# One tile of two transposed whole, two loads held, and the last rows dealt out anew in a kernel for the lower triangles of Gram matrices

## The reference

```python
def reference(r_inputs):                                # (2048, 64, 256) float32
    Z = jnp.einsum('bnd,bmd->bnm', r_inputs, r_inputs)  # 64 x 64 products of rows, for each batch
    li, lj = jnp.tril_indices(64, k=-1)
    return Z[:, li, lj]                                 # (2048, 2016): below the diagonal, row by row
```

## Time and profile before

| | |
|---|---|
| time before, median of 3 runs | 398.48 us (398.1 to 398.72) |
| profiled execution: its own time | 397.29 us |
| profiled execution: span | 395.5 us |
| PE busy | 368.8 us (93%) |
| DVE busy | 370.4 us (94%) |
| ACT, POOL busy | 188.3, 200.3 us (48%, 51%) |
| HBM read and written | 134.22 MB, 16.52 MB: 381 GB/s over the span |

### The profile page before, as it was taken

The page is one execution under the profiler, slowest core; times in us unless marked ns, Lnnn a source line. Parts: engine busy times, 40 slices in busy tenths (PEclk is TensorE's granted clock), DMA queues, the critical chain, the costliest instruction groups (busy, mean ns, idle before and its releaser), DMA issues.

```text
span 395.5 us, 69567 instructions
## 1 busy us (share of the span) xinstructions
PE 368.8 (93%) x33280; PEld 363.7 (92%) x33280; DVE 370.4 (94%) x369; ACT 188.3 (48%) x858; POOL 200.3 (51%) x975
## 2 busy tenths in 40 slices
PE   4389999999999999999999999999999999999960
PEld 4389999999999999999999999999999999999960
DVE  3258899999999999999999999999999999999995
ACT  0021245454545555555555455545554555545572
POOL 2000075482828456382837557282846648282765
PEclk9569999999999999999999999999999999999995
DMA  8999999999999999999999999999999999994307
GB/s 321 423 421 419 423 422 418 380 424 423 416 405 389 427 420 423 398 422 418 411 422 362 426 423 422 416 419 421 413 420 377 427 414 417 385 416 162 114 16 193
DMA packets 21274, 150.99 MB, mean 382 GB/s; under 512 B 2688, under 2 KB 2816, under 8 KB 4864
## 3 DMA queue, kind: packets, MB, share of 16 engines
q1 hardware_dynamic: 18912, 136.81, 85.5%
q10 hardware_dynamic: 2336, 13.94, 8.7%
HBM read 134.22 MB, written 16.52 MB: 381 GB/s over the span
## 4 chain that ended last, share of the span: by engine, by line
DVE 44%; issue 29%; PE 24%; ACT 0%; DVEq 0%; ACTq 0%
DVE x_turned L232 31%; PE bank_set L309 24%; DVE row_halves L249 11%; DVE x_in L256 1%; DVE packed_rows L154 1%; DVE packed_rows L143 0%; ACT packed_rows L143 0%; DVE x_turned L261 0%; DVEq L248 0%; ACT products L336 0%; DVEq L75 0%; DVEq L279 0%; ACTq L332 0%
## 5 line engine op out<-in xcount | busy, mean ns | idle before, releaser
L309 PE MATMUL bank_set<-x_turned 32*64 32x64 f32 x33280 | 368.8, 237 | 13.1 <-issue 11.1
L309 PEld LDWEIGHTS bank_set<-x_turned 32*64 32x64 f32 x33280 | 363.7, 131 | 18.0 <-issue 11.7
L232 DVE STREAM_TRANSPOSE x_turned<-x_in 128x1024 f32<-128x1024 f32 x256 | 295.7, 1207 | 19.3 <-PE bank_set L309 15.6
L154 POOL COPY packed_rows<-row_halves 32x32 f32<-32x32 f32 (+30 forms) x930 | 191.7, 206 | 187.5 <-DVE row_halves L249 149.9
L336 ACT COPY products<-bank_set 128x512 f32<-128x512 f32 x128 | 75.1, 586 | 146.6 <-PE bank_set L309 130.9
L249 DVE STREAM_TRANSPOSE row_halves<-products 128x1024 f32<-128x1024 f32 x60 | 72.2, 1203 | 0.0
L143 ACT COPY packed_rows<-row_halves 128x32 f32<-128x32 f32 (+30 forms) x465 | 61.2, 218 | 12.5 <-DVE row_halves L249 12.3
L149 ACT COPY packed_rows<-row_halves 128x128 f32<-128x128 f32 x240 | 54.1, 300 | 15.0 <-DVE row_halves L249 13.3
L336 ACT ACT_TABLE_LOAD x1 | 1.3, 1283 | 26.0 <-PE bank_set L309 26.0
L154 POOL COPY packed_rows<-x_in 32x32 f32<-32x32 f32 (+30 forms) x31 | 5.0, 212 | 2.2 <-DVE x_in L256 2.2
L256 DVE STREAM_TRANSPOSE x_in<-products 128x512 f32<-128x512 f32 (+1 forms) x5 | 4.6, 995 | 0.0
## 6 DMA issues: line engine op xcount, KB each, us to landing
x_in<-x_dram SPq DMA_DIRECT2D x128, 1024.0 KB, 15.1
y_dram<-packed_rows ACTq DMA_DIRECT2D x20, 504.0 KB, 8.9
y_dram<-packed_rows SPq DMA_DIRECT2D x4, 504.0 KB, 5.0
y_dram<-packed_rows ACTq DMA_DIRECT2D x6, 252.0 KB
y_dram<-packed_rows ACTq DMA_DIRECT2D x24, 63.0 KB
y_dram<-packed_rows SPq DMA_DIRECT2D x1, 380.0 KB
y_dram<-packed_rows ACTq DMA_DIRECT2D x1, 380.0 KB
y_dram<-packed_rows SPq DMA_DIRECT2D x1, 124.0 KB
```

The source lines that it names most:

```text
L154: return copy(packed_rows[first:first + BLOCK, group % 2, :, at + BLOCK:at + i], halves(group)[first + BLOCK:first + HALF, i, :, 0:i - BLOCK])
L232: nc.vector.transpose(x_turned[:, j, chunks].rearrange("p c b s (h u n v) -> p u v (c b s h) n", h=ROWS // BLOCK, u=PAIRS, v=PAIR), x_in[: ...
L309: done = nc.tensor.matmul(bank_sets[j][side * HALF:(side + 1) * HALF, g, slot, :].rearrange("r (n u v) -> r u n v", u=PAIRS, v=PAIR), rows ...
```

## The change

Five edits stand in one diff.

- `PARTIALS` becomes (1, 2): an even tile is turned by one transpose of 2048 elements a partition, and TensorE reads it behind one wait; odd tiles stay in halves.
- `HELD = (3, 4)`: the fourth load waits until tile 0 is turned whole, the fifth until the first half of tile 1 is. The loads behind them on SyncE's queue wait with them.
- `by_few` holds for 9 groups of the 13 that ScalarE stores (all but 0, 4, 8 and 12) in place of 6.
- Behind the last tile ScalarE packs rows 10 to 31, GpSimd rows 5 to 9, VectorE rows 1 to 4. Both sides of the long rows are stored by SyncE; the short rows still leave from SyncE and ScalarE.
- The last tile's copy out of PSUM is split in two, rows 32 to 63 first; the pieces of long rows wait for the first part alone.

```diff
+    HELD = (3, 4)
     LAP = 2
+    PARTIALS = (1, 2)
-    PARTIALS = 2
-    PARTIAL = CHUNKS // PARTIALS
-    LAST_HOME = (GROUPS * PIECES - 2) * 4 + 2
+    BY_POOL = (5, 10)
...
+        def chunks_of(j, h):
+            some = CHUNKS // PARTIALS[j]
+            return range(h * some, (h + 1) * some)
...
+        def wait_last_kept(engine, piece):
+            lap, s = place(TILES - 1)
+            engine.wait_ge(kept[s], (lap + 2) * LAP - (1 if piece < LONG_PIECES else 0))
...
         def by_few(group):
-            return group % 2 == 1 and group <= FEW_UNTIL
+            return group % 4 != 0 and group <= FEW_UNTIL
...
-        def store_last(engine, side):
-            group, long_rows = GROUPS - 1, first_column(BLOCK)
+        def store_last_long(engine):
+            group = GROUPS - 1
             engine.wait_ge(packed_home, group * PIECES + LONG_PIECES)
             engine.wait_ge(packed_across, (group + 1) * LONG_PIECES)
             engine.wait_ge(last_carried, 1)
-            store(engine, group, slice(long_rows, PACKED), WHOLE_SIDES[side:side + 1])
-            engine.wait_ge(packed_home, GROUPS * PIECES - 1)
-            engine.wait_ge(last_packed, 2)
-            store(engine, group, slice(0, long_rows), WHOLE_SIDES[side:side + 1])
+            store(engine, group, slice(first_column(BLOCK), PACKED), WHOLE_SIDES)
+
+        def store_last_short(engine, side):
+            engine.wait_ge(last_packed, 3)
+            store(engine, GROUPS - 1, slice(0, first_column(BLOCK)), WHOLE_SIDES[side:side + 1])
...
                 if t >= IN_RING:
                     lap, j = place(t - IN_RING)
-                    sync.wait_ge(turned[j][PARTIALS - 1], (lap + 1) * LAP)
+                    sync.wait_ge(turned[j][-1], (lap + 1) * LAP)
+                elif t in HELD:
+                    lap, j = place(t - HELD[0])
+                    sync.wait_ge(turned[j][0], (lap + 1) * LAP)
...
-            store_last(sync, 0)
+            store_last_long(sync)
+            store_last_short(sync, 0)
...
-            pool.wait_ge(rows_turned, GROUPS * PIECES - 1)
-            rows = piece_rows(PIECES - 2)
-            for i in range(rows.start + PIECE // 2, rows.stop):
+            pool.wait_ge(rows_turned, GROUPS * PIECES)
+            for i in range(*BY_POOL):
                 last = pack_short(nc.gpsimd.tensor_copy, GROUPS - 1, i)
...
-                for h in range(PARTIALS):
-                    chunks = slice(h * PARTIAL, (h + 1) * PARTIAL)
+                for h in range(PARTIALS[j]):
+                    chunks = slice(chunks_of(j, h).start, chunks_of(j, h).stop)
                     dve.wait_ge(multiplied[j][h], lap)
...
-            for i in range(1, piece_rows(PIECES - 1).stop):
+            for i in range(1, BY_POOL[0]):
                 last = pack_short(nc.vector.tensor_copy, GROUPS - 1, i)
...
-                nc.scalar.copy(
-                    products[:, group % KEPT_RING, :, in_group * PER_SIDE:(in_group + 1) * PER_SIDE].rearrange(
-                        "p i (g b) -> p i g b", b=SLOTS),
-                    bank_sets[s][:, :, 0:SLOTS, :].rearrange("p g b i -> p i g b")).then_inc(kept[s], LAP)
+                by_rows = (slice(0, ROWS),) if t < TILES - 1 else (slice(BLOCK, ROWS), slice(0, BLOCK))
+                for rows in by_rows:
+                    nc.scalar.copy(
...
-            for n in range(n, LAST_HOME):
+            for n in range(n, ((GROUPS - 1) * PIECES + LONG_PIECES) * 4):
                 pack(n)
-            store_last(act, 1)
+            act.wait_ge(rows_turned, GROUPS * PIECES)
+            for i in range(BY_POOL[1], BLOCK):
+                last = pack_short(nc.scalar.copy, GROUPS - 1, i)
+            last.then_inc(last_packed, 1)
+            store_last_short(act, 1)
```

More of the change, by code:

```diff
@@ L98, in gram_lower_triangle @@
         loaded = [semaphore(f"loaded{k}") for k in range(IN_RING)]
-        turned = [[semaphore(f"turned{j}_{h}") for h in range(PARTIALS)] for j in range(LAP)]
+        turned = [[semaphore(f"turned{j}_{h}") for h in range(PARTIALS[j])] for j in range(LAP)]
         kept = [semaphore(f"set_kept{s}") for s in range(SETS)]
-        multiplied = [[semaphore(f"multiplied{j}_{h}") for h in range(PARTIALS)] for j in range(LAP)]
+        multiplied = [[semaphore(f"multiplied{j}_{h}") for h in range(PARTIALS[j])] for j in range(LAP)]
         rows_turned = semaphore("rows_turned")
@@ L203, in _ @@
             for j in range(BLANK):
-                nc.gpsimd.memset(x_turned[:, j, PARTIAL:CHUNKS], 0.0).then_inc(turned[j][1], LAP)
+                nc.gpsimd.memset(x_turned[:, j, CHUNKS // 2:CHUNKS], 0.0).then_inc(turned[j][-1], LAP * PARTIALS[j] // 2)
             for group in range(GROUPS):
@@ L260, in _ @@
             for j in range(BLANK):
-                nc.vector.memset(x_turned[:, j, 0:PARTIAL], 0.0).then_inc(turned[j][0], LAP)
+                nc.vector.memset(x_turned[:, j, 0:CHUNKS // 2], 0.0).then_inc(turned[j][0], LAP * PARTIALS[j] // 2)
             turned_rows = 0
@@ L271, in _ @@
             for run in range(RUNS):
-                wait_kept(dve, (GROUPS - 1) * GROUP_TILES + (run + 1) * GROUP_TILES // RUNS - 1)
                 if run < RUNS - 1:
+                    wait_kept(dve, (GROUPS - 1) * GROUP_TILES + (run + 1) * GROUP_TILES // RUNS - 1)
                     turn_last_rows(run, slice(0, ROWS))
@@ L276, in _ @@
                     for piece in range(PIECES):
+                        wait_last_kept(dve, piece)
                         turn_last_rows(run, piece_rows(piece)).then_inc(rows_turned, 1)
@@ L292, in multiply @@
             def multiply(j):
-                for h in range(PARTIALS):
+                for h in range(PARTIALS[j]):
                     pe.wait_ge(turned[j][h], count)
                     for slot in range(SLOTS):
-                        last_slot = h == PARTIALS - 1 and slot == SLOTS - 1
+                        last_slot = h == PARTIALS[j] - 1 and slot == SLOTS - 1
                         if j == LAP - 1 and last_slot:
                             pe.reg_add(count, count, LAP)
-                        for c in range(h * PARTIAL, (h + 1) * PARTIAL):
+                        for c in chunks_of(j, h):
                             if last_slot and c == CHUNKS - 2:
@@ L331, in keep @@
                 group, in_group = divmod(t, GROUP_TILES)
-                act.wait_ge(multiplied[s][PARTIALS - 1], lap + 1)
+                act.wait_ge(multiplied[s][-1], lap + 1)
                 if group >= KEPT_RING and in_group == 0:
                     act.wait_ge(rows_turned, (group - KEPT_RING + 1) * PIECES)
-                nc.scalar.copy(
-                    products[:, group % KEPT_RING, :, in_group * PER_SIDE:(in_group + 1) * PER_SIDE].rearrange(
-                        "p i (g b) -> p i g b", b=SLOTS),
-                    bank_sets[s][:, :, 0:SLOTS, :].rearrange("p g b i -> p i g b")).then_inc(kept[s], LAP)
+                by_rows = (slice(0, ROWS),) if t < TILES - 1 else (slice(BLOCK, ROWS), slice(0, BLOCK))
+                for rows in by_rows:
+                    nc.scalar.copy(
+                        products[:, group % KEPT_RING, rows, in_group * PER_SIDE:(in_group + 1) * PER_SIDE].rearrange(
+                            "p i (g b) -> p i g b", b=SLOTS),
+                        bank_sets[s][:, :, 0:SLOTS, rows].rearrange("p g b i -> p i g b")).then_inc(
+                        kept[s], LAP // len(by_rows))
             def pack(n):
@@ L354, in pack @@
                         last = pack_long_pair(nc.scalar.copy, group, i)
-                if quarter == 3 or n == LAST_HOME - 1:
+                if quarter == 3:
                     last.then_inc(packed_home, 1)
```

## The result

| | before | after |
|---|---|---|
| median of 5 runs each | 398.25 us (397.66 to 398.72) | 401.87 us (401.37 to 402.11) |
| profiled execution: time, span | 397.29, 395.5 us | 402.11, 400.3 us |
| ratio of the times, 95% interval | | 1.0089 [1.0075, 1.0103] |

The forecast of 402.1 us is met to 0.2. The experiments show that two of its terms were wrong by about as much, in opposite directions, so that the time was met by luck.

A forecast was written before the change was run, and what follows sets the result against it. PE or DVE, whichever is later, sets a lap, with DMA almost the bound at the end. Loads 7.2 us later less 2.8 room, -0.2 laps, -0.6 end: +3.6, median 402.1 us; own range 399.5 to 405.0, with rivals from 396.0.

The forecast's parts named there:

- The path: Loads up to tile 120: 7.2 us later against 2.8 of room, so tile 120 is turned 4.4 us late.
- Held loads: Head of the kernel: load 4 lands at 21.5 instead of 17.0, the stream of loads 4.5 us later, never given back.
- What the quiet buys: TensorE's head: second and third stall each 0.8 us shorter on a quiet DMA, 1.6 us for its start.
- Pieces: Stores of three more groups in pieces: landings 2.7 us later, bounds -3.6 and +5.4.
- Laps: Whole even tiles: 0.04 us saved a lap where VectorE leads, 0.8 in all, -0.2 of it behind tile 120.
- The end: Behind the last tile: short stores start 0.7 us earlier; -0.6 us in all, bounds 0 and -0.9.
- The sum: Whole kernel: loads 4.5 + 2.7 = 7.2 us later, less 2.8 of room, -0.2 and -0.6: +3.6 us.
- room after all: Rival, late loads: the slow engine alone sets landings, so the loads have room; -2.7 us, 395.8 us; chance 0.20.
- pieces free: Rival, stores: pieces cost nothing on the last engine; -0.2 to +0.9, about 398.8 us; chance 0.12.
- buffer 0's circle: Rival, every lap: hand-overs over 0.51 us together make laps longer; +4.1, 402.6 us; chance 0.05.
- The hold doesn't shorten the stalls: Rival, head: TensorE starts as now and loads are later still; costs 0.8 in the forecast, no case of its own.

The follow-up runs named there:

- before_hold: The kernel before plus the held fourth and fifth load, nothing else changed; 396.16 us, 0.9967 of the kernel before.
- no_hold_odd: The kernel after without the held loads and with six groups (the odd ones) in pieces instead of nine; 398.45 us, 1.0015 of the kernel before.
- odd_pieces: The kernel after, held loads kept, with six groups (the odd ones) in pieces instead of nine; 396.44 us, 0.9963 of the kernel before.
- hold_one_odd: The kernel after with six groups (the odd ones) in pieces and the fourth load alone held; 396.17 us, 0.9958 of the kernel before.
- hold_one: The kernel before with the fourth load alone held, the fifth following at once; 395.67 us, 0.9946 of the kernel before.
- no_pieces: The kernel after with no group in pieces, all stores of whole sides; 405.19 us, 1.0186 of the kernel before.

## Why the prediction was right, step by step

- **The path** (loads, through tile 120): right. Tile 120 lands 7.0 us later (forecast 7.2) and is turned 4.6 late (4.4), and VectorE's waits lie at tiles 96 to 118 (85 to 122).
- **Held loads**: the failed step is "Since the queue never ran empty afterwards, nothing gives this back." Load 4 landed 4.1 later, within the bounds, but of that 1.6 was left at tile 120 with six groups in pieces (2.0 in before_hold). A queue that is never empty still lost rate before, where the ring held the loads back.
- **What the quiet buys**: mis-sized, and by another way. 0.8 was taken for the second and third stall each; measured were 2.2 for the second, -0.3 for the third and 0.3 for the first, 2.2 in sum against 1.6. On the kernel before the third fell too, from 3.79 to 2.69; why not here stays open.
- **Pieces**: mis-sized. The forecast took +2.7, with a lead of 2.7 that the four engines had over the slow one; with the hold they had none, and the term was its upper bound, +5.4 (355.7 to 361.1). The parts that reason from bytes (four engines, 142 KB, a fifth that stores slowly) held in every run.
- **Laps**: forecast -0.8, of which -0.2 behind tile 120. From the start of the steady work to TensorE's end no_hold_odd takes 360.8 (22.65 to 383.41), the kernel before 360.6 (21.28 to 381.89). The times agree: with the whole tile and the new end no_hold_odd stands 0.15% above the kernel before, odd_pieces level with before_hold, and hold_one_odd 0.1% above hold_one. The whole tile gives nothing, though VectorE issues fewer instructions.
- **The end**: forecast -0.6, measured -0.1 (13.5 against 13.6 behind TensorE). The last short store is issued at 395.06, the span ends 5.2 later; before, these were 391.2 and 4.3. With both long stores on one queue ahead of it, what the packing saved was waited for in the DMA engines. Which of the two, the one queue or the shared engines, wasn't tried.
- **The sum**: 4.5 + 2.7 = 7.2 stands for 1.6 + 5.4 = 7.0, on the way from before over odd_pieces to after. The total was right because the two errors cancelled: luck, and the time alone would have confirmed a wrong account of the hold. A second error is hidden too. In the two profiled executions the difference is 4.8, not 3.6: 4.6 at tile 120, 0.3 more from there to TensorE's end (24.8 against 24.5) and -0.1 at the end, against 4.4 - 0.2 - 0.6. The medians differ by 3.6 again, since before's profiled execution was a short one (397.29) and after's a long one (402.11).
- **The rivals**: room after all and pieces free are out (tile 120 lands 7.0 late, the pieces cost all of their bytes), buffer 0's circle too. "The hold doesn't shorten the stalls" holds for the third and nearly for the first.

## What to carry to other kernels

Transfers that land when the slowest of many engines is done are planned by counting bytes per engine, and an edit that is good for one engine is priced on the one that is next; here both were level and both moves that were tried lost. A delay at the head costs only what is not going to be lost later anyway: look for the place where the queue is thin, by the time from issue to landing, before carrying a delay through to the end. A total that comes out right proves none of its terms; take the change apart in both directions.

## What the runs showed of the hardware

- One DMA engine of sixteen, by the rule cited above the fifth or sixth, stores a lane of 15.75 KB in 1.0 to 1.3 us, where a lane on the first four cost 0.6; it was late alone (share 0.06 to 0.08) in all five kernels that gave it 52 lanes or more.
- The second stall of TensorE's sequencer in its first pass was 3.7 to 4.2 us where loads ran on and 1.2 to 1.8 in every kernel that held the fourth load; the first (3.4 to 3.7) and the third (2.7 to 4.6) show no such step. What the sequencer waits for in a stall, no row shows.
- TensorE's granted clock fell to 0.50 for some 3 us (311 to 314) after a wait of 1.83 us for a load, and was 0.62 at 363 to 367 in no_pieces behind a stretch with 3.65 busy of 6.00. In the first of these 221 matmuls ran in 3 us, against 303 in the three of the earlier trace rows: a late load can cost more than its wait.
